# The attention's output projection in plain fp32 instead of three fp16 products

## What is computed

```
x = x + 0.5 * ffn(layernorm(x))
x = x + attention(layernorm(x))
x = x + 0.5 * ffn(layernorm(x))

attention(x):                      # 16 heads of 64 features
    Q, K, V = x @ Wq + bq, x @ Wk + bk, x @ Wv + bv
    Qc, Qs = relu(Q) * cos(t), relu(Q) * sin(t)       # and the same for K
    S_cos += kc * v;  S_sin += ks * v                 # running sums over t, per head
    out = (qc @ S_cos + qs @ S_sin) / max(qc . z_cos + qs . z_sin, 1e-6)
    return out @ Wo + bo                              # [.., 1024] @ [1024, 128]
```

## Time and profile before

| | |
|---|---|
| runs, device time | 1248.94, 1246.42, 1245.84 us; median 1246.42 |
| profiled execution, its span from first to last instruction | 1250.3 us; 3.9 above the median (the profile gives no other time of its own) |
| mean granted clock of TensorE | 0.930 of full speed |
| busy, share of the span | PE 929.8 us (74%), DVE 1010.6 (81%), ACT 707.5 (57%), POOL 766.6 (61%) |
| instructions | PE 12872, DVE 2109, ACT 1014, POOL 635 |

### The profile page before, as it was taken

One profiled execution on the slowest core, in us unless ns is written; L12 is line 12 of the kernel. 1 busy time (PEld: TensorE's weight loads), 2 busy tenths in 40 slices (PEclk: granted clock), 3 DMA queues, 4 the chain that ended last, 5 costly groups with the idle time before them and its releaser, 6 DMA issues.

```text
span 1250.3 us, 32918 instructions
## 1 busy us (share of the span) xinstructions
PE 929.8 (74%) x12872; PEld 754.8 (60%) x12872; DVE 1010.6 (81%) x2109; ACT 707.5 (57%) x1014; POOL 766.6 (61%) x635
## 2 busy tenths in 40 slices
PE   3302988878997877887888898977988867969800
PEld 2302987766765655665666666755766656958700
DVE  7887776996889899889899899898898857738933
ACT  2111766646766665665766676755766635746600
POOL 2187736716876665676665655547887921767264
PEclk9999999999999998998998999988999968989955
DMA  9322423310000000000000000000000012334231
GB/s 336 130 110 74 140 77 107 101 55 9 8 9 8 7 7 8 6 9 8 6 8 2 2 2 2 3 1 14 15 14 15 14 43 66 120 98 126 74 93 50
DMA packets 69508, 61.77 MB, mean 49 GB/s; under 512 B 8304, under 2 KB 60016, under 8 KB 69104
## 3 DMA queue, kind: packets, MB, share of 16 engines
q1 hardware_dynamic: 60448, 42.64, 11.1%
q0 software_dynamic: 8192, 16.79, 4.3%
q10 hardware_dynamic: 720, 0.23, 0.1%
HBM read 30.80 MB, written 28.84 MB: 48 GB/s over the span
## 4 chain that ended last, share of the span: by engine, by line
DVE 29%; POOL 24%; PE 21%; issue 16%; ACT 7%; DMA 1%; DVEq 0%; POOLq 0%; SPq 0%
POOL xs L636 8%; POOL arena_a L1377 5%; DVE arena_b L1275 4%; POOL arena_a L1359 4%; DVE arena_a L1233 3%; ACT arena_c L1153 3%; PE bank L1043 3%; DVE arena_c L828 3%; POOL arena_b L665 3%; DVE arena_c L1271 2%; POOL arena_c L1381 2%; DVE xn_new L426 2%; PE bank L967 2%; PE bank L742 2%; DVE arena_b L1258 2%
## 5 line engine op out<-in xcount | busy, mean ns | idle before, releaser
L636 POOL DMA_INDIRECT xs<-xhl,slot_idx x128 | 156.3, 1221 | 89.5 <-issue 57.1
L803 ACT ACTIVATE arena_c<-bank,s_pre 128x1024 f32<-128x1024 f32 x92 | 102.3, 1112 | 158.0 <-PE bank L744 152.8
L1377 POOL TENSOR_TENSOR arena_a<-arena_a 128x1024 f16<-128x1024 f32 x64 | 139.4, 2178 | 53.8 <-ACT arena_a L1153 53.2
L1359 POOL TENSOR_TENSOR arena_a<-arena_b,trig_rows 128x512 f32<-128x512 f32 x128 | 160.2, 1272 | 8.6 <-issue 8.6
L1153 ACT ACTIVATE arena_c<-arena_a 128x1024 f16<-128x1024 f32 x64 | 67.6, 1057 | 160.3 <-DVE arena_a L1233 160.3
L665 POOL DMA_INDIRECT arena_b<-ys,slot_idx x96 | 108.3, 1128 | 68.4 <-DMA ys<-arena_b 40.7
L757 PE MATMUL bank<-wdn_hi,arena_c 128*128 x736 | 131.9, 223 | 22.4 <-DVE arena_c L828 22.4
L828 DVE SCALAR_TENSOR_TENSOR arena_c<-arena_c,s_h 128x1024 f16<-128x1024 f32 x92 | 124.7, 1356 | 23.2 <-ACT arena_c L808 23.2
L758 PE MATMUL bank<-wdn_hi,arena_c 128*128 x736 | 131.9, 223 | 0.0
L759 PE MATMUL bank<-wdn_lo,arena_c 128*128 x736 | 131.9, 223 | 0.0
L1258 DVE TENSOR_TENSOR arena_b<-bank,decay 128x512 f32<-128x512 f32 x128 | 82.4, 686 | 40.5 <-PE bank L1043 40.0
(11 more groups left out here) (227 smaller groups left out, 3728.9 us busy)
## 6 DMA issues: line engine op xcount, KB each, us to landing
arena_b<-xs SPq DMA_DIRECT2D x92, 128.0 KB, 2.5
ys<-arena_b SPq DMA_DIRECT2D x92, 128.0 KB
xs<-arena_c SPq DMA_DIRECT2D x2, 3072.0 KB, 18.4
arena_a<-in_w_up SPq DMA_DIRECT2D x1, 2048.0 KB, 13.0
arena_b<-in_w_down SPq DMA_DIRECT2D x1, 2048.0 KB, 13.5
xs<-xhl,slot_idx POOLq DMA_INDIRECT x128, 2.3
out_x<-x_tok SPq DMA_DIRECT2D x8, 256.0 KB, 2.6
arena_b<-ys,slot_idx POOLq DMA_INDIRECT x96
```

The costliest lines, as they stand in the source:

```text
L636: nc.gpsimd.indirect_dma_start(d["xs"][half], bass.IndirectOffsetOnAxis(slot_idx[:, half, choice, t:t + 1], axis=0), xhl[:, half, t, :], N ...
L1359: i = nc.gpsimd.tensor_tensor(q_trig[h], q_relu[h], trig_rows[:, bass.ds(u * BLK, BLK)], ALU.mult)
L1377: nc.gpsimd.tensor_tensor(q_lo, arena_a[:, 0:2 * BLK], q_hi, ALU.subtract).then_inc(a["q_lo_done"], 1)
```

## The change

Wo is kept in fp32 as one tile `wo`, without scaling. oT is one fp32 tile. copy_out writes it whole; out_low and its semaphore are gone; project_out waits for copy_out and does four fp32 matmuls. In the setup, the largest of Wo, its power of two and its two parts go; one copy of Wo takes their place (part 8), the parts are counted anew, and the reduction on POOL takes one column less. The core of the diff:

```diff
-        wo_hi, wo_lo = sb("wo_hi", [P, NHP, D], F16), sb("wo_lo", [P, NHP, D], F16)
+        wo = sb("wo", [P, NHP, D])
...
-        oT = take(2 * BLK, F16)
+        oT = take(BLK)
...
-                reduce_largest(g, 2, 9, 2)
+                reduce_largest(g, 2, 8, 2)
...
             def project_out(hp, s):
-                pe.wait_ge(a["ot_lo_done"], s + 1)
+                pe.wait_ge(a["ot_copied"], s + 1)
                 for c in range(TPB):
-                    o_t = tuple(oT[:, part * BLK + c * P:part * BLK + (c + 1) * P] for part in range(2))
-
-                    i = three(ps_op[:, c * P:(c + 1) * P], o_t, (wo_hi[:, hp, :], wo_lo[:, hp, :]),
-                              hp == 0 and c == 0, hp == NHP - 1 and c == TPB - 1)
+                    i = nc.tensor.matmul(ps_op[:, c * P:(c + 1) * P], oT[:, c * P:(c + 1) * P], wo[:, hp, :],
+                                         start=(hp == 0 and c == 0), stop=(hp == NHP - 1 and c == TPB - 1),
+                                         skip_group_check=True)
                 i.then_inc(a["op_done"], 1)
...
-                nc.scalar.activation(oT[:, 0:BLK], ps_tr, ACT.Copy).then_inc(a["ot_copied"], 1)
+                nc.scalar.activation(oT, ps_tr, ACT.Copy).then_inc(a["ot_copied"], 1)
...
-            def out_low(s):
-                v.wait_ge(a["ot_copied"], s + 1)
-                nc.vector.tensor_tensor(oT[:, BLK:2 * BLK], ps_tr, oT[:, 0:BLK], ALU.subtract
-                                        ).then_inc(a["ot_lo_done"], 1)
...
-                if hp:
-                    out_low(s - 1)
-                else:
-                    if n > 0:
-                        out_low(last_step(n - 1))
-
                 out = ps_so[:, :, 0:TPB * VZ].rearrange("p h (c z) -> p h c z", c=TPB)
...
-            out_low(last_step(NBLK - 1))
             add_attention(v, NBLK - 1)
...
-                largest_of(v, (2, 3, 4, 8)[j], raw[j], last=(j == 3))
+                largest_of(v, (2, 3, 4)[j], raw[j], last=(j == 2))
...
-                power_of_two(v, W_OUT, largest_all[:, 8:9])
...
-                link(v, nc.vector.tensor_scalar(s_tmp[:, 1:2], pow2[:, W_OUT:W_OUT + 1], 2.0 ** -20, None, ALU.mult))
-                link(v, nc.vector.tensor_tensor(s_att[:], s_tmp[:, 1:2], pow2[:, W_QKV:W_QKV + 1], ALU.mult))
+                link(v, nc.vector.tensor_scalar(s_att[:], pow2[:, W_QKV:W_QKV + 1], 2.0 ** -6, None, ALU.mult))
...
-                link(v, both(wo_hi[:].rearrange("p n d -> p (n d)"), wo_lo[:].rearrange("p n d -> p (n d)"), raw[3], s_outw))
+                link(v, nc.vector.tensor_copy(wo[:].rearrange("p n d -> p (n d)"), raw[3]))
```

More of the change, by code:

```diff
@@ L292, in build @@
                  "s_ready s_hi_done s_lo_done o_done den_step o32_done otr_done "
-                 "ot_copied ot_lo_done op_done att_sum att_x s_zero").split()
+                 "ot_copied op_done att_sum att_x s_zero").split()
         a = {n: sem(n) for n in names}
@@ L1462, in expert_weights_low @@
             nc.vector.scalar_tensor_tensor(lo, raw, s_w[:, col:col + 1], hi, ALU.mult, ALU.subtract).then_inc(ready, 1)
-        ATT_SETUP_SLOTS = ((0, 0), (0, 2), (0, 4), (0, 6), (0, 10), (0, 12), (0, 14),
-                           (1, 0), (1, 6), (1, 8), (1, 10), (1, 12))
-        LINKS, LINKS_BEFORE = 10, (0, 0, 0, 0, 0, 16, 17, 18, 19, 20, 22, 28, 33)
+        ATT_PARTS = 11
+        LINKS, LINKS_BEFORE = 10, (0, 0, 0, 0, 11, 12, 13, 14, 15, 16, 22, 27)
         def attention_weights(v, j):
@@ L1476, in attention_weights @@
             raw = [arena_a[:, i * HD:(i + 1) * HD] for i in range(4)]
-            s_qkvw, s_outw = s_w[:, W_QKV:W_QKV + 1], s_w[:, W_OUT:W_OUT + 1]
+            s_qkvw = s_w[:, W_QKV:W_QKV + 1]
             def both(hi, lo, src, scale):
@@ L1481, in both @@
                 return nc.vector.scalar_tensor_tensor(lo, src, scale, hi, ALU.mult, ALU.subtract)
-            if j < 4:
+            if j < 3:
                 if j == 0:
@@ L1488, in attention_weights @@
                         largest_of(v, col, bias[:])
-                largest_of(v, (2, 3, 4, 8)[j], raw[j], last=(j == 3))
-            elif j == 4:
+                largest_of(v, (2, 3, 4)[j], raw[j], last=(j == 2))
+            elif j == 3:
                 v.wait_ge(max_all, 3)
@@ L1500, in attention_weights @@
                 link(v, nc.vector.tensor_scalar(s_eps[:], s_eps[:], DEN_EPS * CORE, 2.0 ** -100, ALU.mult, ALU.max))
-                link(v, nc.vector.tensor_scalar(s_tmp[:, 1:2], pow2[:, W_OUT:W_OUT + 1], 2.0 ** -20, None, ALU.mult))
-                link(v, nc.vector.tensor_tensor(s_att[:], s_tmp[:, 1:2], pow2[:, W_QKV:W_QKV + 1], ALU.mult))
-            elif j < 7:
-                g = j - 5
+                link(v, nc.vector.tensor_scalar(s_att[:], pow2[:, W_QKV:W_QKV + 1], 2.0 ** -6, None, ALU.mult))
+            elif j < 6:
+                g = j - 4
                 both(wq_hi[:, :, g, :], wq_lo[:, :, g, :], raw[0].rearrange("p (h f) -> p h f", h=H), s_qkvw)
[L1506 to L1509, removed]
-                link(v, both(wo_hi[:].rearrange("p n d -> p (n d)"), wo_lo[:].rearrange("p n d -> p (n d)"), raw[3], s_outw))
+            elif j < 8:
+                hi, lo = ((wk_hi, wk_lo), (wv_hi, wv_lo))[j - 6]
+                both(hi[:], lo[:], raw[j - 5], s_qkvw)
+            elif j == 8:
+                link(v, nc.vector.tensor_copy(wo[:].rearrange("p n d -> p (n d)"), raw[3]))
             else:
@@ L1514, in attention_weights @@
                 link(v, nc.vector.tensor_tensor(part_row[:, 1:2], ident[:, 0:1], ident[:, 1:2], ALU.subtract))
-                i = j - 10
+                i = j - 9
                 bias = (bk_row, bv_row)[i]
@@ L1627, in _ @@
             assert chain[0] == LINKS
-            for j in range(len(ATT_SETUP_SLOTS)):
+            for j in range(ATT_PARTS):
                 attention_weights(v, j)
```

## The result

The changed kernel takes 1252.06 us (median of 20 runs, 1244.83 to 1258.64) against 1246.80 of the kernel before in the same comparison; the ratio is 1.0034, interval 1.0018 to 1.0049. Of the changed kernel's own profiled execution the span is 1253.1 us, 2.8 above that of before.

What follows compares the result with a forecast made beforehand. In the attention it took PE as the bound in plain steps and the chain through v_high on ACT before rest_of_v, not DVE. Terms +3.1 - 0.8 - 1.3 - 0.9 - 0.2 = -0.1 us gave 1246, range 1240 to 1254.

Steps and rivals of the forecast that it cites:

- project_out, +0.09 in 35 steps, +3.1: Attention steps with project_out right behind the V projection: fp32 matmuls delay rest_of_v 0.09 us, +3.1 us in all.
- Rival 1: project_out in v_high's shadow: fp32 weight loads are not hidden, +1.0 us in 35 steps, 1277 us; chance 0.08.
- Half-clock first steps: First steps of blocks 2, 3 and 4: project_out moves out of rest_of_v's way, -0.28 us each, -0.8 together.
- DVE-last steps: Seven attention steps where DVE doesn't wait for the scores: 0.67 us at a batch change, 0.1 elsewhere, -1.3 together.
- Setup: Before the attention: fewer DVE instructions for Wo hold up POOL's scatter less, -0.9 us (between -1.6 and +0.7).
- Handover: After the last attention step, into the second FFN: project_out starts 0.7 us earlier but takes longer, -0.2 us.
- DVE gets 0.67 us per step: Attention, out_low gone: late steps gain all 0.67 us on DVE but wait longer for the scores; only seven steps gain.
- rival 2: Late attention steps: PE runs at half clock more often, five more such steps cost +6 us, 1252 us; chance 0.08.
- Rival 3: Late attention steps: DVE is the bound after all, 28 steps x 0.67 = -19 us, 1228 us; chance 0.08.

Runs made afterwards that it cites:

- e1: The changed kernel plus an unused DVE instruction of about 0.6 us where out_low stood, in all steps; 1248.90 us, 0.9993 of the kernel before.
- e9: The changed kernel plus an unused 0.6 us DVE instruction in the seven hp 1 steps of blocks 1 to 7 alone; 1247.26 us, ratio 0.9982.
- e6: The changed kernel with POOL's finish_power moved from step hp 1 to hp 2; 1243.97 us, 0.9956 of the kernel before.
- e7: The kernel before with POOL's finish_power moved from step hp 1 to hp 2; 1245.72 us, ratio 0.9973.
- e2: The kernel before without out_low, project_out keeping twelve fp16 matmuls with the high part in place of the low; 1246.67 us, ratio 0.9998.
- e8: The changed kernel with one of project_out's four fp32 matmuls moved ahead of the products of q and state; 1248.15 us, ratio 0.9991.
- e11: Second run of the changed kernel with one of four fp32 matmuls moved ahead of the products of q and state; 1248.53 us, ratio 1.0002.

## Why the prediction was wrong

The forecast was no change, 1246; the time is up by 5.3 us in medians, and by the ratio of 1.0034 by 0.34%. The terms, by the step periods and rows of the profiled pair:

- *project_out, +0.09 in 35 steps, +3.1.* 0.09 was right (9.20 to 9.28). It was paid in some 17 steps, +1.5: other steps, as 52 to 56 and 60 to 62, stayed where they were (step 60: 10.50 and 10.50; POOL is busy in 9.80 us of it).
- *Rival 1, loads not hidden:* wrong, records 0.12 us apart. The Trainium skill's rule (TensorE: Matmul & The Clock Gate, "Part 3: Packing small matmuls — row/col tiling"), that loads overlap only between different row groups, did not hold here: loads of 0.19 us on all rows hide in a spacing of 0.12.
- *Half-clock first steps, three times -0.28.* Twice -0.3 (16.35 to 16.04 in blocks 3 and 4), nothing in block 2 (16.02 to 16.04).
- *DVE-last steps, -1.3.* The change of batch gave 0.47 (10.81 to 10.34) and the step behind it 0.24; the others nothing.
- *Setup, -0.9.* PE's first transposes came 0.17 later (114.66), not earlier: the meetings moved along with DVE's stream, their number did not fall.

```profile
102.91 0.69 DVE L1494 COPY wo<-arena_a 128x1024 f32<-128x1024 f32 x1
...
102.14 1.69 POOL L636 DMA_INDIRECT xs<-xhl,slot_idx  x1 [0.30 <-issue]
104.13 0.95 POOL L636 DMA_INDIRECT xs<-xhl,slot_idx  x1 [0.30 <-issue]
...
106.79 1.72 POOL L636 DMA_INDIRECT xs<-xhl,slot_idx  x1 [0.30 <-issue]
```

The copy itself held up no further DMA: 1.69 is what a subtraction alone imposed (1.67 and 1.68 on the two DMAs ahead), 0.95 is undisturbed. So the rule of the Trainium skill's box on SWDGE (SBUF — State Buffer, "SBUF: two separate sides"), which the prediction weighed, was not seen to act on the copy, which ran within one DMA that a subtraction had already held up.

- *Handover, -0.2.* From o32's start to add_attention's it was 1008.29 - 1003.51 = 4.78 and is 4.07, -0.7: the granted clock was 1.00 in project_out, where it was 0.50 in the earlier trace rows. Two rows of before, then three of the changed kernel:

```profile
1003.51 0.69 DVE L1291 TENSOR_TENSOR arena_c<-bank,arena_c 128x512 f32<-128x512 f32 x1
1008.29 0.75 DVE L1351 SCALAR_TENSOR_TENSOR x_tok<-bank,s_att,x_tok 128x512 f32<-128x512 f32 x1 [1.56 <-PE bank L969]
...
1008.93 1.16 PE L1028 MATMUL bank<-wo,arena_c 128*128 128x128 f32 x8 [0.69 <-ACT arena_c L1172]
...
1006.06 0.69 DVE L1279 TENSOR_TENSOR arena_c<-bank,arena_c 128x512 f32<-128x512 f32 x1
1010.13 0.75 DVE L1338 SCALAR_TENSOR_TENSOR x_tok<-bank,s_att,x_tok 128x512 f32<-128x512 f32 x1 [3.37 <-PE bank L1028]
```

These come to about -0.3 (+1.5 - 0.6 - 0.7 + 0.2 - 0.7), near the forecast's -0.1, in part because project_out's overestimate and the setup's miss offset each other. What is missing is no size of these terms, but a cost that had no term. One reading was off without harm: the 62 of the earlier trace rows are 60 weight loads and 2 matmuls of line 1007, not 62 of 64 matmuls.

**The step that failed** is "DVE gets 0.67 us per step. ... In late steps it gains all 0.67, and waits longer for the scores too", priced at nothing. The wait did grow. But DVE's next instructions moved 0.6 us earlier, and I asked only who waits for them, not whom they meet: k_low met POOL's power, and probs_lo of steps 10 and 26 then took 6.75 and 6.77 us, which made these steps 4.8 to 4.9 us longer and blocks 1 to 3 together 5.8. I had met the same thing in the setup, where a DVE subtraction stretched POOL's DMA by 0.7, and did not carry it into the attention, where the two engines share SBUF in every step. The Trainium skill (SBUF — State Buffer, "SBUF: two separate sides") says that a DVE instruction with two SBUF inputs and a GpSimd one take the shared port for the whole instruction and the other blocks; the rows agree (k_low 1.22, and the power behind it 2.05 instead of 1.05).

The time came out as rival 2's 1252, by another way: the attention's clock stayed at 0.95. That 1252.06 lies in the stated 1240 to 1254 is luck for the same reason. Rival 3 is refuted too: late steps (hp 6) last 10.72 before and after. That the profiled pair differs by 2.8 where the medians differ by 5.3 has a likely reason in the pair: the profile of before has a probs_lo of 6.21 us of its own in step 17, which is absent in e1, whose DVE instructions stand in the same places. How often the kernel before has one, its single profile can't say. POOL's trains hold up DVE elsewhere too, in kernels of both kinds: in step 50 the probs_lo of before, e1 and e9 took 7.42 to 7.43 us, and in two of the changed kernel's three profiles a normalization (line 426) took 6.53. The change did not make those.

Shown is what the meeting costs in its two steps, and that the loss goes when probs_lo is no longer held up, reached in three ways with PE's stream the same in all: clearly in e9 and e6, in e1 by the median alone. That more than the loss goes holds for e6 alone, and e6's move helps the kernel before as well (e7). Not settled is how the rest divides: neither edit alone, the missing out_low (e2) nor, with it, the thinner fp32 tail (e8, e11), is measurably slower than before. The likely reading is that the 0.09 us of the fp32 matmuls makes the meeting fall at the same place in every execution; that was not shown.

## What to carry to other kernels

When an instruction goes from an engine that isn't the bound, list what now runs earlier there and what the engine that shares its memory port does at that time: here a start that moved by 0.6 us cost almost 5 in a step. An engine's row that is several times longer than its group's usual one (6.75 us against 1.32) was here a wait in disguise, and it stands in the profile as busy time of that engine. Moving one small instruction out of such a train (finish_power, one step later) was worth more here than the arithmetic saved.

## Not expected of the hardware

- A DVE subtraction with two SBUF inputs, 1.32 us in the kernel before, was held until POOL paused: 6.75 to 6.77 us through q_lo, which began 0.09 us ahead of it, and s_lo and trig_q, which began while it was waiting. A gap of 0.31 us on POOL (e6) let it in.
- 0.08 us of lead was enough to hold the other engine up: k_low at 389.46 made the power of 389.54 take 2.05. Where the two did not overlap (e11: the power from 391.05 to 392.10, k_low from 392.20), the power took 1.05.
- fp32 matmul records of 128x128 with 128 columns start 0.12 us apart, against 0.056 for fp16 ones: four fp32 products cost 1.4 times twelve fp16 ones.
